# Two attention layers and two mixture-of-experts layers on one core: the first attention's values as one full-precision product per half

## The chip, the cores and the metric

The kernel runs on one core of one Trainium2 chip. The metric is the device time of one launch in microseconds (us), taken as the median over several runs.

## What is computed

`x` has 1024 tokens of 128 numbers, the context 6404 rows of 96. Four residual layers follow each other, each behind a layer norm of `x`: attention 0 (one head of 128), a mixture of 8 small experts, attention 1 (8 heads of 64, then an output projection), and a mixture of 32 experts with 4 chosen per token and one shared. What matters here is attention 0:

```python
query = jnp.einsum('bqi,ih->bqh', image_features, Wq) + bq
key = jnp.einsum('bkt,th->bkh', text_features, Wk) + bk
value = jnp.einsum('bkt,th->bkh', text_features, Wv) + bv
scores = jnp.einsum('bqh,bkh->bqk', query, key) * scale
weights = jax.nn.softmax(scores, axis=-1)
attended = jnp.einsum('bqk,bkh->bqh', weights, value)
...
x = x + _L0_xattn_ref(_layernorm(x, axis=-1), ctx_768, ...)
```

## The kernel before, in words

Each engine has its own instruction stream, written out by hand and tied to the others by semaphores; there is no scheduler. The context's 6404 rows are padded to 51 tiles (`TILES`) of 126 keys (`KT`), in 17 chunks (`CHUNKS`) of 3 (`CH`). The 1024 queries are two halves of 512 columns.

**Attention 0** never forms keys or values. The query is carried back through Wk (so a score is a product of a context row of 96 with the carried query), and the probabilities are summed against the context rows themselves plus a column of ones (97 numbers: 96 sums and the denominator). Wv is applied once at the end. Its steps in time:

1. A first pass over all tiles finds each query's maximum, and in its gaps makes the values of attention 1 and writes them to DRAM.
2. The second pass, the subject here (0 to 51 tiles, us 97 to 244 of the trace). For tile `j` of a chunk and each half of 512 queries:
   - `scores0` (L1174): three one-pass products in the reduced format float32r (L1180 to L1182), high and low parts of context and query, into PSUM bank `2j + half`.
   - `exp0` (L577) on ScalarE: the exponential in full float32 into `probs0`; `exp0_hi` (L586): the same exponential again, rounded to float32r, into `p_hi`.
   - `context_rows_hi` (L817) on VectorE: the tile's rows, loaded by the SyncE queue into `vslot`, rounded into `rows_hi`. GpSimd subtracts to `rows_lo` (L467). `probs_lo` (L822) on VectorE: `probs0 - p_hi` into `p_lo`.
   - `attend0` (L1185): three one-pass products, `rows_hi` by `p_hi`, `rows_lo` by `p_hi`, `rows_hi` by `p_lo`, added into banks 6 and 7.
   - `fill0` (L800) copies the keys of the same slot's next tile; the SyncE queue (L380) loads the slot's next rows as soon as `rows_lo` is made.
3. TensorE's order within a chunk is `chunk0` (L1202): scores of tile 2, attend 0, scores of the next chunk's tile 0, attend 1, scores of the next 1, attend 2. So a tile's scores stand two attends and two scores ahead of its own attend.

`p_hi` and `p_lo` have one buffer each for all tiles. They lie in the memory of `q_all2` and `q_shift2`, `rows_hi` and `rows_lo` in that of `wv1_hi` and `wv1_lo`; so the profile calls them `q_all`, `q_shift`, `wv_hi`, `wv_lo`, and `probs0` `probs`.

A float32 matmul of 512 columns is one instruction in the program and two records in the profile; one in float32r or bf16 is one of each.

Behind the pass come the division by the denominator, mixture 0 (us 244 to 296), the first keys and maxima of attention 1 (to us 381), its 8 heads (to us 1350), and mixture 1.

Of the kernel before, what the change touches and what calls it, by code (L numbers as in the profile page):

```python
# [6 lines left out]
F32R = mybir.dt.float32r  # L7
BF16 = mybir.dt.bfloat16
U32 = mybir.dt.uint32
ALU = mybir.AluOpType  # L10
ACT = mybir.ActivationFunctionType
AX = mybir.AxisListType.X

P = 128
TOK = 1024
TT = TOK // P
HALF = TOK // 2
D = 128
KEYS = 6404
CD = 96  # L20
KT = 126
TILES = 51
CH = 3
CHUNKS = TILES // CH
# [96 lines left out]
def build_program(nc, x, ctx_rows, ctx_t, a_wq, a_bq, a_wkt, a_bk, a_wv, a_bv,  # L121
# [4 lines left out]
    with ExitStack() as ctx:  # L126
# [6 lines left out]
        def sems(name, n):  # L133
            return [sem(f"{name}{i}") for i in range(n)]
# [3 lines left out]
        ps = ctx.enter_context(nc.psum_tensor("ps", [P, 8, HALF], F32))  # L138
# [42 lines left out]
        slot_keys, attended = sems("slot_keys", CH), sems("attended", CH)  # L181
        scored, exped = sems("scored", 2 * CH), sems("exped", 2 * CH)
# [5 lines left out]
                                    "o", "out", "rsum", "x"))  # L188


        a_plo0, a_av0 = sems("a_plo0", CH), sems("a_av0", CH)
        a_vkeys = sems("a_vkeys", CH)
        a_cslot, a_vproj, a_vevac, a_vout = (sems(f"a_{n}", CH) for n in ("cslot", "vproj", "vevac", "vout"))

# [11 lines left out]
        c_scored, c_exped, c_attended, c_sum, c_sumd = (  # L206
            sem(f"c_{n}") for n in ("scored", "exped", "attended", "sum", "sumd"))
        c_acc, c_sums, c_rden, c_out, c_x, c_bo = (sem(f"c_{n}") for n in ("acc", "sums", "rden", "out", "x", "bo"))
        a_lo, a_padd = sems("a_lo", CH), sems("a_padd", CH)

        g_step, g_logits, g_exp, g_cw, g_cwt, g_cwtsb, g_spread_ready, g_store = (
            sem(f"g_{n}") for n in ("step", "logits", "exp", "cw", "cwt", "cwtsb", "spread_ready", "store"))
# [33 lines left out]
        with ExitStack() as first:  # L246
            def sb_a(name, shape, dt=F32):
                return first.enter_context(nc.sbuf_tensor(name, shape, dt))

            keys_hl = sb_a("keys_hl", [P, TILES, 2, KT], F32R)  # L250
            kslot = sb_a("kslot", [P, CH, 2, KT], F32R)
            vslot = sb_a("vslot", [KT, CH, P])
            probs0 = sb_a("probs0", [KT, CH, TOK])
            q_max = sb_a("q_max", [P, TOK], F32R)
            q_all2 = sb_a("q_all2", [P, 2, TOK], F32R)
            q_shift2 = sb_a("q_shift2", [P, 2, TOK], F32R)
            q_pad = sb_a("q_pad", [97, TOK], F32R)
            wv1_hi = sb_a("wv1_hi", [P, HEADS * HD], F32R)
            wv1_lo = sb_a("wv1_lo", [P, HEADS * HD], F32R)
            v_stage = sb_a("v_stage", [KT, CH, HALF])  # L260
            chunk_max0 = sb_a("chunk_max0", [P, TT, CHUNKS])
            wq0 = sb_a("wq0", [P, D])
            bq0 = sb_a("bq0", [P, 1])
            wkt0 = sb_a("wkt0", [P, CD + 1])
            wv0 = sb_a("wv0", [CD + 1, D + 1])
            rsum0 = sb_a("rsum0", [P, 4, 2])
            xn2 = sb_a("xn2", [P, TT, D])
            f0w = sb_a("f0w", [P, 3 * 256 + 8 * 3 + 2 + 2 + 8 * 8])
            w2_0 = sb_a("w2_0", [P, G0, D])
            b2_0 = sb_a("b2_0", [E0, D])  # L270
            spread0 = sb_a("spread0", [E0, G0, P])
            mask0 = sb_a("mask0", [P, TT, E0])
# [6 lines left out]
        b1_0 = f0w[:, 792:794]  # L279
        hb0 = f0w[:, 794:796]  # L280
        lg0 = f0w[:, 796:860]
        q_all, q_shift = q_all2[:, 0, :], q_shift2[:, 0, :]
        p_hi, p_lo = q_all2[0:KT, 1, :], q_shift2[0:KT, 1, :]
        rows_hi, rows_lo = (w[0:KT, 0:CH * P].rearrange("p (j c) -> p j c", j=CH)[:, :, 0:CD + 1] for w in (wv1_hi, wv1_lo))

        with ExitStack() as second:
            def sb_b(name, shape, dt=F32):
# [32 lines left out]
        def f32(ap):  # L320
            return ap.bitcast(F32)
# [4 lines left out]
        def cols(half):  # L326
            return slice(half * HALF, (half + 1) * HALF)
# [16 lines left out]
        def _(sp):  # L344
# [26 lines left out]
            with sp.Fori(0, CHUNKS) as g:  # L371
                k1 = sp.snap(g + 1)
# [4 lines left out]
            with sp.Fori(0, CHUNKS - 1) as g:  # L377
                k1 = sp.snap(g + 1)
                for j in range(CH):
                    sp.wait_ge(a_lo[j], k1)  # L380
                    sp.dma_start(vslot[:, j, 0:CD],
                                 crow_v[bass.ds(g * CH + CH + j, 1)].rearrange("a p c -> p (a c)")).then_inc(a_cslot[j], 16)
            for j in range(CH):
# [46 lines left out]
        def _(pool):  # L430
# [25 lines left out]
            pool.tensor_copy(q_shift[0:CD, :], f32(q_max[0:CD, :])).then_inc(a_qcopy, 1)  # L456
            pool.wait_ge(a_qcopy, 1)
            pool.tensor_copy(q_pad[0:CD, :], f32(q_max[0:CD, :])).then_inc(a_qcopy, 1)

            pool.wait_ge(a_qcopy, 2)  # L460
            with pool.Fori(0, CHUNKS) as g:
                vkeys = pool.snap(g + (CHUNKS + 1))
                k1 = pool.snap(g + 1)
                for j in range(CH):
                    pool.wait_ge(a_vkeys[j], vkeys)
                    pool.wait_ge(a_lo[(j - 1) % CH], k1 if j else g)
                    pool.tensor_tensor(rows_lo[:, j, :], vslot[:, j, 0:CD + 1], f32(rows_hi[:, j, :]),  # L467
                                       ALU.subtract).then_inc(a_lo[j], 1)

            pool.wait_ge(attended[CH - 1], CHUNKS)  # L470

# [55 lines left out]
        def _(act):  # L527
# [38 lines left out]
            with act.Fori(0, CHUNKS - 1) as g:  # L566
                k1 = act.snap(g + 1)
# [7 lines left out]
                v_evac(j, CHUNKS, 16 * (CHUNKS - 1))  # L575

            def exp0(jj, kv, kp):  # L577

                act.wait_ge(a_padd[jj], kp)
                act.wait_ge(a_plo0[jj], kp)  # L580
                for half in range(2):
                    u = 2 * jj + half
                    act.wait_ge(scored[u], kv)
                    act.activation(probs0[:, jj, cols(half)], ps[0:KT, u, :], ACT.Exp, scale=float(D) ** -0.5)  # L584

            def exp0_hi(jj, kv, kp):  # L586

                for half in range(2):
                    u = 2 * jj + half
                    act.wait_ge((a_av0, attended)[half][(jj - 1) % CH], kv if jj else kp)  # L590
                    act.activation(p_hi[:, cols(half)], ps[0:KT, u, :], ACT.Exp,  # L591
                                   scale=float(D) ** -0.5).then_inc(exped[u], 1)

            def exp_tiles(k, k1, k2):
                exp0(1, k1, k)
                exp0_hi(0, k1, k)
                exp0(2, k1, k)
                exp0_hi(1, k1, k)
                if k2 is not None:
                    exp0(0, k2, k1)  # L600
                exp0_hi(2, k1, k)

            exp0(0, 1, 0)
            with act.Fori(0, CHUNKS - 1) as g:
                exp_tiles(g, act.snap(g + 1), act.snap(g + 2))
            exp_tiles(CHUNKS - 1, CHUNKS, None)
            act.wait_ge(attended[CH - 1], CHUNKS)
            act.copy(o0[:, 0:HALF], ps[0:CD + 1, 6, :]).then_inc(a_o, 1)

# [147 lines left out]
        def _(dve):  # L757
# [56 lines left out]
            dve.tensor_tensor(halves(q_shift[CD:CD + 1, :]), ps[CD:CD + 1, 3:5, :], halves(f32(q_max[CD:CD + 1, :])),  # L814
                              ALU.add).then_inc(shifted, 1)

            def context_rows_hi(j, k, k16):  # L817
                dve.wait_ge(a_cslot[j], k16)
                dve.wait_ge(attended[j], k)
                dve.tensor_copy(rows_hi[:, j, :], vslot[:, j, 0:CD + 1]).then_inc(a_vkeys[j], 1)  # L820

            def probs_lo(j, k1):  # L822
                for half in range(2):
                    dve.wait_ge(exped[2 * j + half], k1)
                    dve.tensor_tensor(p_lo[:, cols(half)], probs0[:, j, cols(half)], f32(p_hi[:, cols(half)]),  # L825
                                      ALU.subtract).then_inc((a_plo0, a_padd)[half][j], 1)

            with dve.Fori(0, CHUNKS - 1) as g:
                k1 = dve.snap(g + 1)
                n1 = dve.snap(g * CH + CH)  # L830
                k16 = dve.snap(g * 16 + 16)
                for j in range(CH):
                    context_rows_hi(j, g, k16)
                    probs_lo(j, k1)
                    dve.wait_ge(scored[2 * j + 1], k1)
                    fill0(n1 + j, j)
            for j in range(CH):
                context_rows_hi(j, CHUNKS - 1, 16 * CHUNKS)
                probs_lo(j, CHUNKS)
            dve.wait_ge(attended[CH - 1], CHUNKS)  # L840
            dve.tensor_copy(o0[:, HALF:TOK], ps[0:CD + 1, 7, :]).then_inc(a_o, 1)

# [277 lines left out]
        def _(pe):  # L1120
# [61 lines left out]
                    pe.matmul(s, kslot[0:CD + 1, jj, 1, :], q_pad[0:CD + 1, cols(half)], start=False,  # L1182
                              stop=True).then_inc(scored[u], 1)

            def attend0(j, k1):  # L1185

                pe.wait_ge(a_lo[j], k1)
                for half in range(2):
                    o = ps[0:CD + 1, 6 + half, :]
                    pe.wait_ge((a_plo0, a_padd)[half][j], k1)  # L1190
                    pe.matmul(o, rows_hi[:, j, :], p_hi[:, cols(half)], start=False, stop=False, skip_group_check=True)  # L1191
                    pe.matmul(o, rows_lo[:, j, :], p_hi[:, cols(half)], start=False, stop=False, skip_group_check=True)  # L1192
                    pe.matmul(o, rows_hi[:, j, :], p_lo[:, cols(half)], start=False, stop=False,  # L1193
                              skip_group_check=True).then_inc((a_av0, attended)[half][j], 1)

            pe.wait_ge(shifted, 1)
            pe.wait_ge(a_qcopy, 2)
# [1 line left out]
            pe.wait_ge(a_vevac[CH - 1], CHUNKS)  # L1199


            def chunk0(k, k1, k2):  # L1202
                scores0(2, k1, k)
                attend0(0, k1)
                if k2 is not None:
                    scores0(0, k2, k1)
                attend0(1, k1)
                if k2 is not None:
                    scores0(1, k2, k1)
                attend0(2, k1)  # L1210

            scores0(0, 1, 0)
            scores0(1, 1, 0)
            with pe.Fori(0, CHUNKS - 1) as g:
                chunk0(g, pe.snap(g + 1), pe.snap(g + 2))
            chunk0(CHUNKS - 1, CHUNKS, None)
            pe.wait_ge(a_o, 2)
            for t in range(TT):
                ins = pe.matmul(ps[:, t % 4, (t // 4) * 256:(t // 4) * 256 + D + 1], o0[:, tile_cols(t)], wv0[:, :],
# [383 lines left out]
```

## Time and profile before

| | |
|---|---|
| median of 3 runs | 1484.18 us (1483.55 to 1486.12) |
| the profiled execution's own time | 1484.28 us |
| its span in the profile | 1482.5 us (1.8 us lie around it) |
| TensorE busy | 1396.7 us, 94% of the span |
| VectorE, ScalarE, GpSimd busy | 1111.0, 807.6, 938.7 us |
| mean granted TensorE clock | 0.949 of full speed |
| the pass in question, us 97 to 244 | 147.0 us: TensorE busy 143.3, ScalarE 123.1, VectorE 87.1, GpSimd 20.8 |

A busy matmul record is longer than the time that it keeps the next one waiting, since the next streams in while it drains: the pace of a run of matmuls is the distance between their starts. The shares are averages over stages; what a change in one stage is worth is read in that stage. The granted clock is a share of full speed: 1.00 is 2.4 GHz, 0.50 is 1.2 GHz.

### The profile page before, as it was taken

To read this page: it belongs to the slowest core of one execution; us is meant where nothing else is said; L and a number is where in the kernel's file an instruction comes from. 1 tells how busy PE (TensorE), PEld (TensorE's weight loads), DVE (VectorE), ACT (ScalarE), POOL (GpSimd) and SP (SyncE) were. 2 spreads that over 40 slices of the span, in tenths; PEclk is the share of its full clock that TensorE was granted. 3 is DMA by queue.
4 is the path that set the end of the run, shared out by engine and by line. 5 is a ranking of instruction groups with operands and counts; after the bars stand their busy time and mean duration, and the time that the engine had idled before them with its cause. 6 is when DMAs were issued, how large, how long until landed. Compare 5 with 4: busy or idle time off the path is not lost.

```text
span 1482.5 us, 20192 instructions
## 1 busy us (share of the span) xinstructions
PE 1396.7 (94%) x6199; PEld 791.9 (53%) x6199; DVE 1111.0 (75%) x1518; ACT 807.6 (54%) x1625; POOL 938.7 (63%) x512
## 2 busy tenths in 40 slices
PE   4989996878999999999999999999999999997798
PEld 2867774533455545554555555555555555554465
DVE  6976567479779688778868877887887886766755
ACT  3768884232556556555655655665555555454232
POOL 5001115022689888978988898898898899885110
PEclk9999998565899999999999999999999999998799
DMA  6640000040000200020020011002002000000011
GB/s 158 208 134 17 17 17 7 1 91 2 1 1 1 49 1 1 1 49 1 1 48 1 1 28 22 0 1 49 0 1 45 1 1 1 1 1 13 19 37 39
DMA packets 77371, 39.42 MB, mean 27 GB/s; under 512 B 62047, under 2 KB 70000, under 8 KB 77002
## 3 DMA queue, kind: packets, MB, share of 16 engines
q1 hardware_dynamic: 77290, 38.36, 10.5%
q8 instruction: 49, 0.80, 0.2%
q14 instruction: 32, 0.26, 0.1%
HBM read 24.66 MB, written 13.68 MB: 26 GB/s over the span
## 4 chain that ended last, share of the span: by engine, by line
PE 86%; DVE 7%; DMA 3%; ACT 2%; issue 1%; POOL 0%; SPq 0%; ACTq 0%; DVEq 0%; POOLq 0%
PE ps L1348 24%; PE ps L1335 14%; PE ps L1336 12%; PE ps L1301 9%; PE ps L1288 3%; DMA v_scratch<-v_stage 2%; DVE chunk_max L921 2%; PE ps L1491 2%; PE ps L1191 2%; PE ps L1192 2%; PE ps L1193 2%; PE ps L1182 2%; PE ps L1180 2%; PE ps L1181 2%; PE ps L1280 1%
## 5 line engine op out<-in xcount | busy, mean ns | idle before, releaser
L506 POOL TENSOR_TENSOR psums<-psums,probs 126x1024 f32<-126x1024 f32 (+1 forms) x392 | 820.9, 2094 | 123.4 <-ACT probs L689 74.5
L689 ACT ACTIVATE probs<-ps 126x512 f32<-126x512 f32 (+1 forms) x816 | 416.4, 617 | 273.4 <-PE ps L1336 267.5
L921 DVE TENSOR_REDUCE chunk_max<-ps 128x2 f32<-128x1008 f32 (+1 forms) x416 | 472.9, 1180 | 79.5 <-PE ps L1301 77.9
L1348 PE MATMUL ps<-probs,v_mem 126*64 126x512 f32 (+1 forms) x1632 | 389.7, 598 | 0.0
L1335 PE MATMUL ps<-q_heads,ring 128*126 128x512 f32 (+1 forms) x816 | 342.9, 420 | 1.2
L1336 PE MATMUL ps<-q_low,ring 128*126 128x512 f32 (+1 forms) x816 | 322.5, 395 | 0.0
L974 DVE TENSOR_TENSOR xn<-xn,probs 126x512 f32<-126x512 f32 x126 | 230.6, 1830 | 29.9 <-ACT probs L689 25.6
L648 ACT CAST ring<-ps 64x252 fp32r<-64x252 f32 (+1 forms) x356 | 128.3, 360 | 135.9 <-PE ps L1288 132.8
L1348 PEld LDWEIGHTS ps<-probs,v_mem 126*64 126x64 f32 (+1 forms) x1632 | 111.5, 136 | 165.4 <-issue 121.2
L1335 PEld LDWEIGHTS ps<-q_heads,ring 128*126 128x126 f32 (+1 forms) x816 | 152.1, 186 | 88.8 <-issue 44.2
L1301 PE MATMUL ps<-ring,q_heads 64*128 64x504 f32 (+1 forms) x416 | 168.5, 477 | 15.8 <-DVE chunk_max L921 6.7
L1336 PEld LDWEIGHTS ps<-q_low,ring 128*126 128x126 f32 (+1 forms) x816 | 152.9, 187 | 32.6 <-issue 2.9
L1301 PE MATMUL ps<-ring,q_low 64*128 64x504 f32 (+1 forms) x416 | 168.5, 477 | 0.0
L1301 PEld LDWEIGHTS ps<-ring,q_heads 64*128 64x128 f32 x416 | 70.8, 197 | 159.1 <-issue 70.9
L467 POOL TENSOR_TENSOR wv_lo<-vslot,wv_hi 126x97 fp32r<-126x97 f32 x51 | 20.4, 399 | 190.7 <-DVE wv_hi L820 190.7
L825 DVE TENSOR_TENSOR q_shift<-probs,q_all 126x512 fp32r<-126x512 f32 x102 | 70.5, 692 | 58.8 <-ACT q_all L591 58.6
L911 DVE TENSOR_TENSOR ring<-ps,ring 64x252 fp32r<-64x252 f32 (+1 forms) x178 | 73.7, 414 | 34.6 <-ACT ring L648 32.4
L1301 PEld LDWEIGHTS ps<-ring,q_low 64*128 64x128 f32 x416 | 70.7, 197 | 0.0
L591 ACT ACTIVATE q_all<-ps 126x512 fp32r<-126x512 f32 x102 | 60.9, 599 | 11.1 <-PE ps L1193 1.4
L584 ACT ACTIVATE probs<-ps 126x512 f32<-126x512 f32 x102 | 60.7, 600 | 9.7 <-PE ps L1182 2.9
L515 POOL TENSOR_TENSOR parts<-pair_w,parts 128x256 fp32r<-128x256 f32 x17 | 11.7, 693 | 83.4 <-ACT parts L715 83.4
L795 DVE TENSOR_REDUCE chunk_max<-ps 128x1 f32<-128x378 f32 x136 | 62.7, 539 | 2.0 <-PE ps L1153 2.0
(200 smaller groups left out, 1456.7 us busy)
## 6 DMA issues: line engine op xcount, KB each, us to landing
v_scratch<-v_stage SPq DMA_DIRECT2D x51, 252.0 KB
v_mem<-v_scratch SPq DMA_DIRECT2D x8, 1606.5 KB
ctx_mem<-in_ctx_t SPq DMA_DIRECT2D x3, 803.2 KB, 9.3
vslot<-in_ctx_rows SPq DMA_DIRECT2D x51, 47.2 KB
pair_w<-in_f_pairs SPq DMA_DIRECT2D x17, 128.0 KB, 2.1
pair_w<-in_f_pairs SPq DMA_DIRECT2D x17, 65.0 KB, 1.8
x_tok<-in_x SPq DMA_DIRECT2D x1, 512.0 KB, 3.6
wo<-in_c_wo SPq DMA_DIRECT2D x1, 512.0 KB
```

The costliest lines, as they stand in the source:

```text
L506: pool.tensor_tensor(sums[0:r, 0:width], sums[0:r, 0:width], probs[0:r, n % PROBS, 0:width], ALU.add).then_inc(c_sum, 1)
L648: ins = act.copy(ring[half * HD:(half + 1) * HD, g % RING, tiles, 0, :], ps[part * HD:(part + 1) * HD, bank, 0:(tiles.stop - tiles.start) ...
L689: act.activation(probs[0:r, n % PROBS, cols(half)], ps[0:r, score_bank(t, half), :], ACT.Exp, scale=float(HD) ** -0.5).then_inc(c_exped, 1)
L795: dve.tensor_reduce(chunk_max0[:, i, g:g + 1], ps[:, i % 4, 0:CK], AX, ALU.max).then_inc(max_reduced, 1)
L825: dve.tensor_tensor(p_lo[:, cols(half)], probs0[:, j, cols(half)], f32(p_hi[:, cols(half)]), ALU.subtract).then_inc((a_plo0, a_padd)[half] ...
L911: ins = dve.tensor_tensor(ring[HD:P, g % RING, tiles, 1, :], ps[rows, bank, 0:(tiles.stop - tiles.start) * KT] .rearrange("p (n k) -> p n ...
L921: dve.tensor_reduce(chunk_max[:, h % 2, i:i + 2, c], ps[:, banks[0]:banks[1] + 1, 0:group_tiles(c) * KT], AX, ALU.max).then_inc(c_reduced, 1)
L974: dve.tensor_tensor(sums[0:r, :], sums[0:r, :], new[0:r, :], ALU.add).then_inc(c_sumd, 1)
L1301: pe.matmul(ps[:, banks[half], 0:group_tiles(c) * KT], q[rows, h % 3, tile_cols(i + half)], ring[rows, g % RING, 0:group_tiles(c), 0, :], ...
L1335: pe.matmul(s, ring[:, g % RING, j, 0, 0:r], q_heads[:, h % 3, cols(half)], start=True, stop=False)
L1336: pe.matmul(s, ring[:, g % RING, j, 1, 0:r], q_low[:, h % 3, cols(half)], start=False, stop=True).then_inc(c_scored, 1)
L1348: ins = pe.matmul(ps[half * HD:(half + 1) * HD, B_ACC, :], v_tiles[0:r, h % 2, t, :], probs[0:r, n % PROBS, cols(half)], start=(t == 0), s ...
```

## The change

The parts are gone. `attend0` is one float32 product per half, of `vslot` as loaded and `probs0` as the exponential left it. ScalarE takes each exponential once. VectorE's two roundings and subtractions per tile and GpSimd's subtraction go, with six sets of semaphores. The queue's reload of a slot now waits for that slot's `attended` where it waited for `a_lo`, and TensorE waits for the load itself (`a_cslot`) and for `exped`.

```diff
             with sp.Fori(0, CHUNKS - 1) as g:
                 for j in range(CH):
-                    sp.wait_ge(a_lo[j], k1)
+                    sp.wait_ge(attended[j], k1)
                     sp.dma_start(vslot[:, j, 0:CD], ...
...
-            with pool.Fori(0, CHUNKS) as g:
-                for j in range(CH):
-                    pool.wait_ge(a_vkeys[j], vkeys)
-                    pool.wait_ge(a_lo[(j - 1) % CH], k1 if j else g)
-                    pool.tensor_tensor(rows_lo[:, j, :], vslot[:, j, 0:CD + 1], f32(rows_hi[:, j, :]),
-                                       ALU.subtract).then_inc(a_lo[j], 1)
...
             def exp0(jj, kv, kp):
-                act.wait_ge(a_padd[jj], kp)
-                act.wait_ge(a_plo0[jj], kp)
+                act.wait_ge(attended[jj], kp)
                 for half in range(2):
                     u = 2 * jj + half
                     act.wait_ge(scored[u], kv)
-                    act.activation(probs0[:, jj, cols(half)], ps[0:KT, u, :], ACT.Exp, scale=float(D) ** -0.5)
-            def exp0_hi(jj, kv, kp):
-                for half in range(2):
-                    act.wait_ge((a_av0, attended)[half][(jj - 1) % CH], kv if jj else kp)
-                    act.activation(p_hi[:, cols(half)], ps[0:KT, u, :], ACT.Exp,
+                    act.activation(probs0[:, jj, cols(half)], ps[0:KT, u, :], ACT.Exp,
                                    scale=float(D) ** -0.5).then_inc(exped[u], 1)
...
-            exp0(0, 1, 0)
-            with act.Fori(0, CHUNKS - 1) as g:
-                exp_tiles(g, act.snap(g + 1), act.snap(g + 2))
-            exp_tiles(CHUNKS - 1, CHUNKS, None)
+            with act.Fori(0, CHUNKS) as g:
+                k1 = act.snap(g + 1)
+                for j in range(CH):
+                    exp0(j, k1, g)
...
                 for j in range(CH):
-                    context_rows_hi(j, g, k16)
-                    probs_lo(j, k1)
                     dve.wait_ge(scored[2 * j + 1], k1)
                     fill0(n1 + j, j)
...
-            def attend0(j, k1):
-                pe.wait_ge(a_lo[j], k1)
+            def attend0(j, k1, k16):
+                pe.wait_ge(a_cslot[j], k16)
                 for half in range(2):
-                    o = ps[0:CD + 1, 6 + half, :]
-                    pe.wait_ge((a_plo0, a_padd)[half][j], k1)
-                    pe.matmul(o, rows_hi[:, j, :], p_hi[:, cols(half)], start=False, stop=False, skip_group_check=True)
-                    pe.matmul(o, rows_lo[:, j, :], p_hi[:, cols(half)], start=False, stop=False, skip_group_check=True)
-                    pe.matmul(o, rows_hi[:, j, :], p_lo[:, cols(half)], start=False, stop=False,
-                              skip_group_check=True).then_inc((a_av0, attended)[half][j], 1)
+                    pe.wait_ge(exped[2 * j + half], k1)
+                    ins = pe.matmul(ps[0:CD + 1, 6 + half, :], vslot[:, j, 0:CD + 1], probs0[:, j, cols(half)], start=False,
+                                    stop=False, skip_group_check=True)
+                ins.then_inc(attended[j], 1)
```

On TensorE, in the loop over chunks, the first attend of a chunk stood so before (between the scores of tile 2 and those of the next chunk's tile 0; `q_all` is `p_hi`, `q_shift` is `p_lo`, in brackets the semaphores waited for):

```order
L1191 MATMUL ps<-q_all,wv_hi 97x512 [waits a_plo00,a_lo0]
L1192 MATMUL ps<-q_all,wv_lo 97x512
L1193 MATMUL ps<-q_shift,wv_hi 97x512
L1191 MATMUL ps<-q_all,wv_hi 97x512 [waits a_padd0]
L1192 MATMUL ps<-q_all,wv_lo 97x512
L1193 MATMUL ps<-q_shift,wv_hi 97x512
```

and so with the change, scores of tile 2's second half ahead of it and the next scores behind:

```order
L1130 MATMUL ps<-q_shift,kslot 126x512 [waits exped5]
L1131 MATMUL ps<-q_all,kslot 126x512
L1132 MATMUL ps<-q_pad,kslot 126x512
L1136 ISA
L1139 MATMUL ps<-probs,vslot 97x512 [waits exped0,a_cslot0]
L1139 MATMUL ps<-probs,vslot 97x512 [waits exped1]
L1125 REGISTER_ALU
L1130 MATMUL ps<-q_shift,kslot 126x512 [waits exped0,slot_keys0]
```

Six matmuls of one attend have become two; the order of scores and attends is the same.

On ScalarE, before, from the end of the first pass into the loop (`L604` is the loop's head, the rows of L584 write `probs0`, those of L591 `p_hi`):

```order
L584 ACT_TABLE_LOAD
L584 ACTIVATE probs<-ps 126x512 x2
L604 UNCONDITIONAL_BRANCH
L583 REGISTER_ALU
L584 ACTIVATE probs<-ps 126x512 x2
L591 ACTIVATE q_all<-ps 126x512 x2
L584 ACTIVATE probs<-ps 126x512 x2
L591 ACTIVATE q_all<-ps 126x512 x2
```

and with the change, from the loop's head to its branch back:

```order
L570 UNCONDITIONAL_BRANCH
L566 REGISTER_ALU
L567 ACT_TABLE_LOAD
L567 ACTIVATE probs<-ps 126x512 x6
L570 REGISTER_ALU
L570 COMPARE_AND_BRANCH
```

Twelve exponentials per chunk have become six, and the load of the exponential's table has moved from ahead of the loop into it.

## Rows read from the trace of the kernel before

**Rows 1.** Stretches of the second pass: us, each engine's busy us (records), clock, DMA.
```profile
97.00:244.00 147.00, 143.33 (x612) 106.61 (x612) 87.05 (x203) 123.11 (x206) 20.78 (x52) 1.00 0.07 16
...
103.10:238.70 135.60, 135.59 (x582) 101.47 (x582) 82.44 (x195) 116.09 (x195) 19.56 (x49) 1.00 0.07 17
```
**Rows 2.** Groups by line, us 97 to 244: busy us, mean ns, then idle before.
```profile
L825 DVE TENSOR_TENSOR q_shift<-probs,q_all 126x512 fp32r<-126x512 f32 x102 | 70.5, 692 | 58.8 <-ACT q_all L591 58.6
L591 ACT ACTIVATE q_all<-ps 126x512 fp32r<-126x512 f32 x102 | 60.9, 599 | 11.1 <-PE ps L1193 1.4
L584 ACT ACTIVATE probs<-ps 126x512 f32<-126x512 f32 x102 | 60.7, 600 | 9.7 <-PE ps L1182 2.9
...
L1180 PE MATMUL ps<-q_shift,kslot 97*126 97x512 f32 x102 | 40.3, 395 | 1.6 <-DVE q_shift L814 1.6
L1191 PE MATMUL ps<-q_all,wv_hi 126*97 126x512 f32 x102 | 40.3, 395 | 2.9 <-DVE q_shift L825 2.9
...
L467 POOL TENSOR_TENSOR wv_lo<-vslot,wv_hi 126x97 fp32r<-126x97 f32 x51 | 20.4, 399 | 190.7 <-DVE wv_hi L820 190.7
```
**Rows 3.** Instructions in order of time, TensorE, first products of attends: start us, us.
```profile
111.43 0.39 PE L1191 MATMUL ps<-q_all,wv_hi 126*97 126x512 f32 x1
...
225.96 0.39 PE L1191 MATMUL ps<-q_all,wv_hi 126*97 126x512 f32 x1
...
228.75 0.39 PE L1191 MATMUL ps<-q_all,wv_hi 126*97 126x512 f32 x1
```
**Rows 4.** The same view, TensorE in mixture 1's loop: L1491 is float32.
```profile
1421.07 0.39 PE L1486 MATMUL ps<-cw,spread 96*128 96x512 bf16 x1
1421.30 1.02 PE L1491 MATMUL ps<-hgate,pair_w 128*128 128x512 f32 x2
...
1422.40 0.40 PE L1479 MATMUL ps<-parts 128*128 128x512 f32 x1
...
1428.73 1.02 PE L1491 MATMUL ps<-hgate,pair_w 128*128 128x512 f32 x2
```
**Rows 5.** The same view, TensorE in attention 1's last head.
```profile
1316.76 3.65 PE L1348 MATMUL ps<-probs,v_mem 126*64 126x512 f32 x16
...
1324.25 1.08 PE L1348 MATMUL ps<-probs,v_mem 126*64 126x512 f32 x4
```
**Rows 6.** Waits in the pass (total, times, longest); then its start in order of time.
```profile
PE ps L1191 <- DVE q_shift L825: 2.9, 3, 1.3
...
98.31 1.28 ACT L584 ACT_TABLE_LOAD   x1 [3.68 <-PE ps L1182]
...
99.61 2.06 ACT L584 ACTIVATE probs<-ps 126x512 f32<-126x512 f32 x4
...
101.31 0.39 PE L1182 MATMUL ps<-q_pad,kslot 97*126 97x512 f32 x1
```
**Rows 7.** DMA issues of the page: count, KB each, median us to landing.
```profile
wq<-in_c_wq SPq DMA_DIRECT2D x8, 64.0 KB, 9.6
...
wk<-in_c_wk SPq DMA_DIRECT2D x8, 48.0 KB, 2.9
```
**Rows 8.** Stretches behind the pass, TensorE: us, busy (records), granted clock, DMA.
```profile
272.00:279.00 7.00, 6.55 (x21) 0.99 0.01 1
...
327.00:381.00 54.00, 47.24 (x110) 0.50 0.01 1
381.00:1350.00 969.00, 962.06 (x4574) 1.00 0.06 12
```
**Rows 9.** The chain that ended last, behind the pass: start us, us.
```profile
268.79 3.54 PE ps L1243 x4
...
273.21 1.72 PE ps L1243 x4
...
279.41 1.22 PE ps L1261 x4
...
293.75 0.74 PE ps L1262 x2
```

More of the change, by code:

```diff
@@ L188, in build_program @@
                                     "o", "out", "rsum", "x"))
-        a_plo0, a_av0 = sems("a_plo0", CH), sems("a_av0", CH)
         a_vkeys = sems("a_vkeys", CH)
@@ L208, in build_program @@
         c_acc, c_sums, c_rden, c_out, c_x, c_bo = (sem(f"c_{n}") for n in ("acc", "sums", "rden", "out", "x", "bo"))
-        a_lo, a_padd = sems("a_lo", CH), sems("a_padd", CH)
         g_step, g_logits, g_exp, g_cw, g_cwt, g_cwtsb, g_spread_ready, g_store = (
@@ L254, in build_program @@
             q_max = sb_a("q_max", [P, TOK], F32R)
-            q_all2 = sb_a("q_all2", [P, 2, TOK], F32R)
-            q_shift2 = sb_a("q_shift2", [P, 2, TOK], F32R)
+            q_all = sb_a("q_all", [P, TOK], F32R)
+            q_shift = sb_a("q_shift", [P, TOK], F32R)
             q_pad = sb_a("q_pad", [97, TOK], F32R)
@@ L281, in build_program @@
         lg0 = f0w[:, 796:860]
-        q_all, q_shift = q_all2[:, 0, :], q_shift2[:, 0, :]
-        p_hi, p_lo = q_all2[0:KT, 1, :], q_shift2[0:KT, 1, :]
-        rows_hi, rows_lo = (w[0:KT, 0:CH * P].rearrange("p (j c) -> p j c", j=CH)[:, :, 0:CD + 1] for w in (wv1_hi, wv1_lo))
         with ExitStack() as second:
@@ L458, in _ @@
             pool.tensor_copy(q_pad[0:CD, :], f32(q_max[0:CD, :])).then_inc(a_qcopy, 1)
-            pool.wait_ge(a_qcopy, 2)
-            with pool.Fori(0, CHUNKS) as g:
-                vkeys = pool.snap(g + (CHUNKS + 1))
-                k1 = pool.snap(g + 1)
-                for j in range(CH):
-                    pool.wait_ge(a_vkeys[j], vkeys)
-                    pool.wait_ge(a_lo[(j - 1) % CH], k1 if j else g)
-                    pool.tensor_tensor(rows_lo[:, j, :], vslot[:, j, 0:CD + 1], f32(rows_hi[:, j, :]),
-                                       ALU.subtract).then_inc(a_lo[j], 1)
             pool.wait_ge(attended[CH - 1], CHUNKS)
@@ L583, in exp0 @@
                     act.wait_ge(scored[u], kv)
-                    act.activation(probs0[:, jj, cols(half)], ps[0:KT, u, :], ACT.Exp, scale=float(D) ** -0.5)
-            def exp0_hi(jj, kv, kp):
-                for half in range(2):
-                    u = 2 * jj + half
-                    act.wait_ge((a_av0, attended)[half][(jj - 1) % CH], kv if jj else kp)
-                    act.activation(p_hi[:, cols(half)], ps[0:KT, u, :], ACT.Exp,
-                                   scale=float(D) ** -0.5).then_inc(exped[u], 1)
[L594 to L601, printed above, removed]
-            exp0(0, 1, 0)
-            with act.Fori(0, CHUNKS - 1) as g:
-                exp_tiles(g, act.snap(g + 1), act.snap(g + 2))
-            exp_tiles(CHUNKS - 1, CHUNKS, None)
+                    act.activation(probs0[:, jj, cols(half)], ps[0:KT, u, :], ACT.Exp,
+                                   scale=float(D) ** -0.5).then_inc(exped[u], 1)
+            with act.Fori(0, CHUNKS) as g:
+                k1 = act.snap(g + 1)
+                for j in range(CH):
+                    exp0(j, k1, g)
             act.wait_ge(attended[CH - 1], CHUNKS)
@@ L815, in _ @@
                               ALU.add).then_inc(shifted, 1)
[L817 to L826, printed above, removed]
             with dve.Fori(0, CHUNKS - 1) as g:
@@ L830, in _ @@
                 n1 = dve.snap(g * CH + CH)
-                k16 = dve.snap(g * 16 + 16)
                 for j in range(CH):
-                    context_rows_hi(j, g, k16)
-                    probs_lo(j, k1)
                     dve.wait_ge(scored[2 * j + 1], k1)
                     fill0(n1 + j, j)
-            for j in range(CH):
-                context_rows_hi(j, CHUNKS - 1, 16 * CHUNKS)
-                probs_lo(j, CHUNKS)
             dve.wait_ge(attended[CH - 1], CHUNKS)
@@ L1199, in _, with chunk0 @@
             pe.wait_ge(a_vevac[CH - 1], CHUNKS)
-            def chunk0(k, k1, k2):
+            def chunk0(k, k1, k2, k16):
                 scores0(2, k1, k)
-                attend0(0, k1)
+                attend0(0, k1, k16)
                 if k2 is not None:
                     scores0(0, k2, k1)
-                attend0(1, k1)
+                attend0(1, k1, k16)
                 if k2 is not None:
                     scores0(1, k2, k1)
-                attend0(2, k1)
+                attend0(2, k1, k16)
             scores0(0, 1, 0)
@@ L1214, in _ @@
             with pe.Fori(0, CHUNKS - 1) as g:
-                chunk0(g, pe.snap(g + 1), pe.snap(g + 2))
-            chunk0(CHUNKS - 1, CHUNKS, None)
+                chunk0(g, pe.snap(g + 1), pe.snap(g + 2), pe.snap(g * 16 + 16))
+            chunk0(CHUNKS - 1, CHUNKS, None, 16 * CHUNKS)
             pe.wait_ge(a_o, 2)
```

## The prediction

> **What bounds the kernel now.** I read the stretches of the program first. From us 97 to 244, the only part that the diff touches, TensorE is busy 143.3 of 147.0 us at a granted clock of 1.00; in the inner 135.6 us it is busy 135.59 [rows 1]. ScalarE has 123.1 and VectorE 87.1 in the same stretch, so both have air, GpSimd nearly all. The groups by line then say why ScalarE is that full: 102 exponentials at 600 ns, twice [rows 2]. But those are work beside TensorE's, and what ends last is a matmul. The order of time gives TensorE's pace: the first products of two following attends start at 225.96 and 228.75, 2.79 us apart, and 111.43 to 225.96 is 114.53 us for 41 tiles, 2.793 us each [rows 3]. A tile is 12 one-pass products of 512 columns, so one costs 2.793 / 12 = 0.2328 us. (The 395 ns of the groups [rows 2] hold the drain, which the next product covers.) A pass with no gap at one product per 0.233 us is bound by the count of products, and by nothing that ScalarE, VectorE or GpSimd do.
>
> **The change, part by part.**
>
> *The three products of a half become one float32 product.* Removed per tile: 6 x 0.2328 = 1.397 us of TensorE. Added: two float32 products of 512 columns. The trace has the price in the loop of mixture 1, at full clock: L1491 is one float32 matmul, two records. From its start at 1421.30 to the same at 1428.73 are three rounds, 2.477 us each, and a round has 7 one-pass products and this one [rows 4]: 2.477 - 7 x 0.2328 = 0.85 us, entry and exit included. It is no cheaper than 3.6 one-pass products, where the change takes out 3. The other place is attention 1: eight float32 matmuls in four pairs, a pair side by side in the two column halves of the array, then 16 one-pass products; block to block is 1324.25 - 1316.76 = 7.49 us [rows 5]. That leaves 7.49 - 16 x 0.2328 = 3.77 us, 0.94 per pair, with what it costs to change between half and full columns. Nothing in the trace has exactly 126 rows by 97 columns in float32 at full clock. Bounds are therefore 0.85 and 0.94. I take 0.85: L1491 uses the whole array, as the new product does, has one-pass products on both sides, as here, and the new product splits no columns.
> Per tile 2 x 0.85 - 1.397 = +0.303 us; over 51 tiles **+15.5 us**, all on the path since TensorE has no gap there. (With 0.94: +24.7 us.)
>
> The Trainium skill, "Perfetto Trace Analysis", section Engine Utilization, gives TensorE's output rate as halved for its FP32_LOW_HIGH; read as the whole price of a float32 product, it would make one cost two one-pass products, and the sum would be below zero (rival B). Its page "FP8 and Floating Point Precision", TensorE Precision Notes, says true FP32 takes four passes through the array; at the pace above that is 4 x 0.2328 = 0.93 us, and the sum would be some +20.8 us; the row of 0.85 stands under it and is used.
>
> *The gaps at the ends.* TensorE waits for `p_lo` three times, 2.9 us in all: once in the first attend, where the last score product starts at 101.31 and the attend not before 103.03, and twice among the last three tiles, where no scores stand between [rows 6]. After the change the first attend needs the rows (loaded long before) and two exponentials. The table load starts at 98.31, the exponentials at 99.61, two take 1.3 us, and so they are done by 100.9, before the last score product is through. In the last chunk an attend of 1.7 us is longer than the two exponentials of the next tile. Both gaps go: **-2.9 us**.
>
> *ScalarE.* 102 exponentials of 0.60 us less. Added: the table load is inside the loop now, 17 times instead of once, 1.28 us each [rows 6]. A chunk then has 1.28 + 6 x 0.65 = 5.2 us of ScalarE against 3 x 3.10 = 9.3 us of TensorE. The load comes behind the wait for the slot's `attended`, ahead of tile 0's exponentials. TensorE needs those after two attends and two groups of scores, 2 x 1.7 + 2 x 1.4 = 6.2 us from the end of tile 0's scores; load and two exponentials are 2.6 us, with one earlier exponential ahead 3.2. Hidden, 3 us to spare: 0. Without that cover it would be 16 x 1.28 = 20.5 us.
>
> *VectorE and GpSimd.* 70.5 us of `p_lo`, the roundings of rows, 20.4 us of `rows_lo` [rows 2], all beside TensorE: 0. VectorE's `fill0` no longer stands behind `p_lo`, so keys come earlier. GpSimd goes straight to its wait for the last attend.
>
> *The rows' load.* It was issued when `rows_lo` was made, ahead of the attend; now when the attend is through, and TensorE waits for its landing. The slot is wanted again 9.3 - 1.7 = 7.6 us after its attend ends, less about 0.4 us for the queue's issue: it must land within 7.2 us. The trace has no landing for these 47 KB. The nearest rows are 48 KB in 2.9 us and 64 KB in 9.6 us [rows 7]; the latter are issued around loads of 1.6 MB, of which the pass has none (DMA share 0.07 [rows 1]). I take 2.9: hidden, 0. By 9.6 it would be rival C.
>
> *Behind the pass.* Nothing is changed, but it begins some 13 us later, and TensorE's clock there comes and goes: 0.99 in us 272 to 279, 0.50 in 327 to 381, 1.00 from 381 on [rows 8]. The same four records of L1243 are 3.54 us at the lower level (1.2 GHz) and 1.72 at the upper (2.4 GHz) [rows 9]. Where the clock rises need not move with the work. Lost, the fast stretch would cost some 6 us; had the small matmuls from 279.41 to 294.5 [rows 9] been fast, some 7 us would be gained. I take 0 and keep -7 and +6 for the range.
>
> Sum against the profiled execution: 1484.28 + 15.5 - 2.9 = 1496.9, say **1497.0 us**. That execution lies 0.1 us from the median of the runs, so nothing is corrected. About 0.2% (3 us) is what a measurement of this kernel can tell from no change.
>
> **The rivals.**
>
> B, *the float32 product is cheap*: one costs two one-pass products (0.47 us), as the half rate named above would have it. A tile falls from 12 to 10 products of 0.2328 us: 51 x -0.466 = -23.7, with the gaps -26.6: 1457.7 us. This is the case on the other side. It decides where a float32 product costs under 0.70 us, three one-pass ones. For it speaks only that every other engine would let it happen (ScalarE 5.2 us per chunk). Against: two records per matmul and 0.85 us [rows 4], and 3.77 us for four pairs [rows 5]. 2%.
>
> C, *the rows land late*: at 9.6 us a slot's turn is 1.7 + 0.4 + 9.6 = 11.7 us instead of 9.3, over 16 chunks +38 us: about 1535. It decides from a landing of 7.2 us. Against it the DMA engines stand nearly idle. 2%.
>
> D, *dearer change of kind*: the price of attention 1's blocks, 0.94 us, holds here. +24.7 - 2.9 = +21.8: 1506.1 us. For it: that block has the 126 rows and `probs` as moving operand, as here. Against: its halves of columns. 9%.
>
> E, *the clock behind the pass pays it back*: it must give 9.6 us or more for no change; even the fast small matmuls give only 7. It would take those and parts of us 327 to 381, where VectorE bounds half of the chain. Time about 1487, or less: 3%, of which I count 2 within 0.2% and 1 beyond.
>
> That the change does not do what it says can be left out: the order of TensorE has two matmuls for six. The forecast itself has 84%.
>
> **How the numbers follow.** Predicted is the likeliest case, 1497.0. Downwards the clock gives up to 5 us within the range, as a full 7 is unlikely; upwards D's price ends at 1506. So 1492 to 1506 leaves out B, C, E and the joint worst of D and clock, under 2 in 10. Faster by over 0.2%: B and a part of E, 3%. Within 0.2%: 2%. Slower by over 0.2%: 95%.
>
> **What would show it.** In the changed profile: 102 float32 products of `probs` and `vslot` in 204 records; first records of following attends 3.10 us apart, 9.3 us per chunk; the pass from us 97 to about 256; no TensorE idle before an attend; ScalarE with 17 table loads and about 83 us busy in the pass; VectorE some 15 us, GpSimd none. A round of 3.28 us is D, of 3.9 us with a wait for `vslot` is C, of 2.33 is B. If the round is 3.10 and the total is off by more than 3 us, the time lies behind the pass, in the rows of the granted clock. A wait for ScalarE once per chunk would be the table load.

## The result, and the profile after

The change takes 1500.41 us (median of 4 runs, 1498.9 to 1501.85) against 1484.76 us before (median of 4, 1483.55 to 1486.12). The ratio is 1.0097, with a 95% interval of 1.0080 to 1.0114: slower by 1%. The forecast was 1497.0 us, in a range of 1492 to 1506.

The groups by line of the changed kernel, us 97 to 262 (busy us, mean ns of a record, idle before and what ended it), answer to [rows 2]:

```profile
L1139 PE MATMUL ps<-probs,vslot 126*97 126x512 f32 x204 | 95.6, 591 | 0.0
L1130 PE MATMUL ps<-q_shift,kslot 97*126 97x512 f32 x102 | 59.7, 585 | 1.6 <-DVE q_shift L781 1.6
L567 ACT ACTIVATE probs<-ps 126x512 f32<-126x512 f32 x102 | 59.2, 596 | 57.4 <-PE ps L1132 55.7
...
L567 ACT ACT_TABLE_LOAD x17 | 21.8, 1283 | 19.0 <-PE ps L1139 18.9
```

102 float32 products in 204 records, 17 table loads, and no idle time of TensorE before an attend. The stretches (us; TensorE, its weight loads, VectorE, ScalarE, GpSimd busy; clock; DMA) answer to [rows 1]:

```profile
103.10:250.00 146.90, 146.90 (x472) 84.03 (x471) 13.45 (x46) 75.22 (x112) 0.00 (x0) 1.00 0.07 16
...
97.00:262.00 165.00, 161.90 (x533) 93.22 (x530) 18.12 (x58) 82.04 (x121) 3.80 (x2) 1.00 0.07 17
```

In the inner stretch TensorE is without a gap, as before. Over the whole window VectorE fell from 87.1 to 18.1 us and ScalarE from 123.1 to 82.0, and GpSimd has nothing left in the inner stretch; none of it made the round shorter. (The window, us 97 to 262, holds 4 us behind the pass.) The order of time, TensorE and one table load on ScalarE, answers to [rows 3]:

```profile
226.69 1.28 ACT L567 ACT_TABLE_LOAD   x1 [1.18 <-PE ps L1139]
...
227.82 1.88 PE L1139 MATMUL ps<-probs,vslot 126*97 126x512 f32 x4
227.98 1.09 ACT L567 ACTIVATE probs<-ps 126x512 f32<-126x512 f32 x2
...
229.14 0.80 PE L1130 MATMUL ps<-q_shift,kslot 97*126 97x512 f32 x1
229.78 0.40 PE L1131 MATMUL ps<-q_all,kslot 96*126 96x512 f32 x1
...
230.94 1.88 PE L1139 MATMUL ps<-probs,vslot 126*97 126x512 f32 x4
...
237.17 1.88 PE L1139 MATMUL ps<-probs,vslot 126*97 126x512 f32 x4
```

Attends start at 227.82, 230.94, (234.06) and 237.17: 9.35 us for three tiles, 3.117 each, where it was 2.793. Less six one-pass products, 1.397, that leaves 1.720 for two float32 products: **0.860 us each**. The first score product behind an attend has a long record (0.80 us): it starts at 229.14, while the attend's records still run (to 227.82 + 1.88 = 229.70), and the next product follows 0.64 us behind it, not 0.23. So part of the float32 product's time stands in that record, and the 585 ns a record of L1130's group are no cost of its own.

### The profile page after: what moved, and what is told of

It is laid out like the page before. It is cut to its first block, busy times and chain, and to the rows that moved or that the text cites. A ratio compares the mean times of both kernels' runs of the same rounds, so it can differ in the third digit from the quotient of the medians.

```text
span 1497.1 us, 19515 instructions
## 1 busy us (share of the span) xinstructions
PE 1412.1 (94%) x6097; PEld 776.6 (52%) x6097; DVE 1035.3 (69%) x1365; ACT 764.8 (51%) x1539; POOL 919.8 (61%) x461
## 4 chain that ended last, share of the span: by engine, by line
PE 87%; DVE 8%; DMA 3%; ACT 2%; issue 1%; POOL 0%; SPq 0%; ACTq 0%; DVEq 0%; POOLq 0%
PE ps L1295 24%; PE ps L1282 14%; PE ps L1283 12%; PE ps L1248 9%; PE ps L1139 6%; PE ps L1235 2%; DMA v_scratch<-v_stage 2%; DVE chunk_max L871 2%; PE ps L1438 2%; PE ps L1130 2%; PE ps L1132 2%; PE ps L1131 2%; PE ps L1227 1%; PE ps L1220 1%; PE ps L1427 1%
## 5 line engine op out<-in xcount | busy, mean ns | idle before, releaser
L1248 PEld LDWEIGHTS ps<-ring,q_heads 64*128 64x128 f32 x416 | 70.7, 197 | 159.3 <-issue 69.3
L768 DVE CAST kslot<-keys_hl 97x252 fp32r (+1 forms) x51 | 14.7, 292 | 131.2 <-PE ps L1132 131.2
L1139 PE MATMUL ps<-probs,vslot 126*97 126x512 f32 x204 | 95.6, 591 | 0.0
```

The costliest lines, as they stand in the source:

```text
L1139: ins = pe.matmul(ps[0:CD + 1, 6 + half, :], vslot[:, j, 0:CD + 1], probs0[:, j, cols(half)], start=False, stop=False, skip_group_check=True)
L1248: pe.matmul(ps[:, banks[half], 0:group_tiles(c) * KT], q[rows, h % 3, tile_cols(i + half)], ring[rows, g % RING, 0:group_tiles(c), 0, :], ...
```

## The experiments

For every profile the table gives the pass, from its first score product to the copy of its sum out of PSUM, and the rest of the span, all in us. The medians of the group from change_again to three_products stand against 1486.13 us of the kernel before, run beside them, those of the group from late_reload on against 1485.97.

| kernel | pass starts | length | rest of the span | median us |
|---|---|---|---|---|
| before | 97.2 | 146.3 | 1336.2 | 1484.76 |
| the change | 98.8 | 159.3 | 1337.8 | 1500.41 |
| change_again | 99.2 | 159.3 | 1338.1 | 1500.57 |
| product_only | 98.8 | 163.4 | 1337.8 | 1502.38 |
| load_hoisted | 97.7 | 159.3 | 1338.8 | 1499.29 |
| three_products | 99.6 | 204.9 | 1340.8 | 1546.63 |
| late_reload | 98.6 | 199.9 | 1339.8 | 1541.54 (one run) |
| two_one_pass | 99.4 | 119.0 | 1337.1 | 1459.71 |
| one_one_pass | 98.4 | 95.2 | 1336.2 | 1434.23 |
| one_one_pass_hoisted | 99.3 | 95.2 | 1337.2 | 1434.54 |

**The product alone.** From the kernel before:

```diff
-                    pe.matmul(o, rows_hi[:, j, :], p_hi[:, cols(half)], start=False, stop=False, skip_group_check=True)
-                    pe.matmul(o, rows_lo[:, j, :], p_hi[:, cols(half)], start=False, stop=False, skip_group_check=True)
-                    pe.matmul(o, rows_hi[:, j, :], p_lo[:, cols(half)], start=False, stop=False,
+                    pe.matmul(o, vslot[:, j, 0:CD + 1], probs0[:, j, cols(half)], start=False, stop=False,
...
```

and the queue's reload waits for `attended[j]`. The other engines go on making the parts, which nothing uses.

> The kernel before with the float32 product alone: both exponentials, the roundings and the subtractions on ScalarE, VectorE and GpSimd stay and the order of waits too; only the parts' three products per half become one float32 product, and the rows' reload waits for the attend. Theory 1 (TensorE's stream alone sets the pass): 51 x 2 x (0.858 - 0.698) = +16.3 us, and of the 2.9 us of gaps some 2.5 stay: about +16 us against the kernel before, a round of 3.12 us per tile. Theory 2 (part of the cost comes from the thinner waits, the table load or the load that is waited for, and the other engines' relief is worth something): clearly other than +16, either under +10 or over +20. The output is that of the change; the parts are computed and not used.

Measured: ratio to before 1.0105 (1.0088 to 1.0122), +16.3 us between medians. The round is 3.12 us, since attends start at 227.05, 230.16 and 233.28 us, in the order of time of TensorE:

```profile
227.05 1.88 PE L1191 MATMUL ps<-probs,vslot 126*97 126x512 f32 x4
230.16 1.88 PE L1191 MATMUL ps<-probs,vslot 126*97 126x512 f32 x4
233.28 1.88 PE L1191 MATMUL ps<-probs,vslot 126*97 126x512 f32 x4
...
257.63 1.93 PE L1191 MATMUL ps<-probs,vslot 126*97 126x512 f32 x4 [0.65 <-DVE q_shift L825]
260.21 1.93 PE L1191 MATMUL ps<-probs,vslot 126*97 126x512 f32 x4 [0.65 <-DVE q_shift L825]
```

The last two rows are gaps of [rows 6], 0.65 us each now; with the first attend's 0.59 the idle time is 1.9 us, not the 2.5 expected. What the gaps cost is more, counted from start to start: the last score product starts at 104.43 and the attend at 105.41, 0.75 us more than a product takes, and the last three attends start 2.52 and 2.58 us apart where two float32 products are 1.72. Together that is 2.4 us. So the product alone makes the whole loss and more, and all the work taken from the three other engines is worth only these gaps. The pass is 4.1 us longer than the change's: 2.4 are the gaps, and 1.6 lie at its start, where the granted clock was low (last section). Between the medians are 1.8 us.

**A third product.** In the change, the first half's product is issued twice, which doubles its sum and its denominator alike:

```diff
                     pe.wait_ge(exped[2 * j + half], k1)
-                    ins = pe.matmul(ps[0:CD + 1, 6 + half, :], vslot[:, j, 0:CD + 1], probs0[:, j, cols(half)], start=False,
-                                    stop=False, skip_group_check=True)
+                    for again in range(2 - half):
+                        ins = pe.matmul(ps[0:CD + 1, 6 + half, :], vslot[:, j, 0:CD + 1], probs0[:, j, cols(half)],
+                                        start=False, stop=False, skip_group_check=True)
```

> The change with the first half's float32 product issued twice per tile (its sum is then doubled, so the output is another). It prices one float32 product in its place. Theory 1: 51 x 0.858 = +43.8 us against the change, a round of 3.97 us. Theory 2 (the price holds a cost of changing between float32r and float32, 0.19 us per tile, which a product more doesn't pay): a further product costs 0.853 or less while the pair costs more than 1.72 us together. Rival price 0.94: +48 us.

Measured: +46.1 us between the medians of this and of change_again. The order of time, TensorE, gives the price free of what lies around the loop:

```profile
224.90 2.74 PE L1140 MATMUL ps<-probs,vslot 126*97 126x512 f32 x6
...
228.87 2.74 PE L1140 MATMUL ps<-probs,vslot 126*97 126x512 f32 x6
...
232.85 1.45 PE L1140 MATMUL ps<-probs,vslot 126*97 126x512 f32 x3
```

A round is 3.975 us (232.85 is the next attend's start), 0.858 more than with two: the third product costs as much as each of the first two. There is no cost of changing between the formats in the pair, and rival D falls: its 0.94 us does not hold here. That it belongs to attention 1's column halves is likely, and was not tried. Of the 46.1 us 43.8 are the rounds; the pass is 45.6 longer, with a stretch of low clock at its start (some 1.6 us), which the change's profiles do not have.

**The table load outside the loop.** In the change:

```diff
-            with act.Fori(0, CHUNKS) as g:
-                k1 = act.snap(g + 1)
-                for j in range(CH):
-                    exp0(j, k1, g)
+            exp0(0, 1, 0)
+            with act.Fori(0, CHUNKS - 1) as g:
+                k1 = act.snap(g + 1)
+                exp0(1, k1, g)
+                exp0(2, k1, g)
+                exp0(0, act.snap(g + 2), k1)
+            exp0(1, CHUNKS, CHUNKS - 1)
+            exp0(2, CHUNKS, CHUNKS - 1)
```

> The change with the first exponential taken out of ScalarE's loop, so that the exponential's table is loaded once and not 17 times. Theory 1 (the load is hidden, 3 us to spare): equal to the change within 1 us, round 3.12 us per tile, ScalarE 20.5 us less busy. Theory 2 (once per chunk the load delays an attend): up to 16 x 1.28 = 20 us less than the change.

Measured: 1499.29 against 1500.57 us of change_again. That is 1.3 us where 1 was expected at most, and within the runs' own spread (1497.34 to 1502.11 here); in the profiles the pass is 159.3 us, the same to the tenth, and starts 1.1 to 1.5 us earlier than in the two of the change. The load was hidden.

**The change again.**

> The change as it is, for the spread of its runs and for the start of the second pass, which its first profile had 1.55 us later (98.80 against 97.25 us). If the late start is chance among the writes of the values in the first pass, this profile's start lies anywhere from 97 to 99 us and the ratio to before comes to 1.0085 to 1.0105. If it belongs to the change, the start is 98.5 to 99 again.

Measured: 1500.57 us, ratio 1.0118 (1.0079 to 1.0158). One of its six runs took 1518.84 us and lifts the ratio above what was expected; between the medians are 14.4 us, 1.0097. The pass starts at 99.18 us and is 159.3 long. The start is 0.18 us later than either expectation allowed, and so fits neither. Over all ten profiles, whose first pass is the same code, the start lies anywhere from 97.2 to 99.6 us; load_hoisted, which is the change but for the table load, starts at 97.7, and other kernels than the change start late too. So the late start does not belong to the change. What goes with it is the granted clock in us 28 to 40, long before the pass that the edits touch (us, TensorE busy, clock, DMA), here before and in the change:

```profile
28.00:40.00 12.00, 11.21 (x46) 0.86 0.36 118
...
28.00:40.00 12.00, 11.91 (x44) 0.76 0.34 112
```

The four profiles with 0.86 there (before, load_hoisted, late_reload, one_one_pass) start the pass at 97.2 to 98.6 us, the six with 0.72 to 0.76 at 98.8 to 99.6. That one makes the other was not tried. The one profile of before had the earliest start of the ten.

**A late reload.** In the change, a slot's reload waits two attends longer:

```diff
-                k1 = sp.snap(g + 1)
+                k1, k2 = sp.snap(g + 1), sp.snap(g + 2)
                 for j in range(CH):
-                    sp.wait_ge(attended[j], k1)
+                    sp.wait_ge(attended[(j + 2) % CH], k2 if j else k1)
```

> The change with a slot's reload issued only after the attend of the slot used last before it, two attends later than in the change. The rows then land on TensorE's path every tile, and the wait shows how long a load of 47 KB takes. A tile is 1.72 us of attend, some 0.45 us of the queue's issue and the landing. Theory 1 (as 48 KB in 2.9 us): about 5.1 us per tile, 48 x 2.0 = +95 us against the change, so that in the change the rows land over 4 us before they are wanted. Rival C (as 64 KB in 9.6 us): 11.8 us per tile, +415 us, and the change would then have waited for its rows. Nothing is left out.

Measured in a single run: 1541.54 us, a pass 40.6 us longer. The order of time shows one turn: the attend before ends at 227.44 + 0.59 = 228.03, the queue issues at 228.23 (the row holds that issue and the next three), TensorE starts on the rows at 229.98 and had waited for the DMA:

```profile
227.44 0.59 PE L1139 MATMUL ps<-probs,vslot 126*97 126x512 f32 x1
...
228.23 12.02 SPq L376 DMA_DIRECT2D vslot<-in_ctx_rows  x4
...
229.98 1.96 PE L1139 MATMUL ps<-probs,vslot 126*97 126x512 f32 x4 [0.54 <-DMA vslot<-in_ctx_rows]
...
233.88 1.96 PE L1139 MATMUL ps<-probs,vslot 126*97 126x512 f32 x4 [0.55 <-DMA vslot<-in_ctx_rows]
```

From issue to use are 1.75 us, and a tile is 3.90 us. That is shorter than either bound I had (2.9 and 9.6 us of landing), so where +95 us was expected it came to +41. In the change the rows have 7.6 us and need some 2: they are over 5 us early, and rival C falls.

**Fewer products.** From the kernel before: the exponential once, as in the change, but written as float32r; `probs_lo` gone; `rows_hi` and `rows_lo` kept; and in `attend0`

```diff
                 for half in range(2):
                     pe.wait_ge(exped[2 * j + half], k1)
                     ins = pe.matmul(ps[0:CD + 1, 6 + half, :], rows_hi[:, j, :], probs0[:, j, cols(half)], ...
+                    ins = pe.matmul(ps[0:CD + 1, 6 + half, :], rows_lo[:, j, :], probs0[:, j, cols(half)], ...
                 ins.then_inc(attended[j], 1)
```

with the added line in two_one_pass and without it in one_one_pass. Both are other computations than before: the first leaves out the probabilities' low part, the second the rows' as well.

> From the kernel before: one exponential per half, rounded to float32r as it is written; rows in high and low part as before; the attend is two one-pass products per half (high rows, low rows), without the probabilities' low part. That low part is left out of the computation, in numerator and denominator alike. Theory 1 (only TensorE's count of streamed columns): 10 products a tile, 2.33 us, 51 x -0.466 = -23.7 and -2.9 of gaps, 1458 to 1460 us. Theory 2 (something else of the change holds the pass near 3.1 us a tile, ScalarE's chain or the rows): no faster than the change, about 1500.

> As two_one_pass, with only the product of the high rows by the rounded probabilities: 8 products a tile. Both low parts are left out of the computation. Theory 1: 1.86 us a tile, 51 x -0.931 = -47.5 and -2.9 of gaps, about 1435 us. Rival: ScalarE, with the table load in its loop 5.2 us per chunk against TensorE's 5.6, begins to hold the pass; then TensorE shows idle before an attend once per chunk and the time lies 5 to 20 us above 1435.

> As one_one_pass, with the first exponential outside ScalarE's loop, so one table load instead of 17. If the load is hidden there too, equal within 1 us; if it holds the pass, this one is up to 16 x 1.28 = 20 us faster than one_one_pass.

Measured: two_one_pass 1459.71 us, ratio to before 0.9828 (0.9810 to 0.9847); one_one_pass 1434.23, ratio 0.9652 (0.9635 to 0.9669); hoisted 1434.54, ratio 0.9663 (0.9637 to 0.9689). The stretch of two_one_pass's whole pass, and two attends of one_one_pass with a table load between them (order of time):

```profile
99.40:218.40 119.00, 118.95 (x510) 90.46 (x510) 24.72 (x100) 79.80 (x119) 20.28 (x51) 1.00 0.09 20
```

```profile
152.88 0.62 PE L1164 MATMUL ps<-probs,wv_hi 126*97 126x512 f32 x2
...
153.69 1.28 ACT L582 ACT_TABLE_LOAD   x1
...
154.75 0.63 PE L1164 MATMUL ps<-probs,wv_hi 126*97 126x512 f32 x2
```

The passes are 119.0 and 95.2 us. By the count, 51 x 10 and 51 x 8 products of 0.2328 us are 118.7 and 95.0, so the pass has nothing left but TensorE's stream, and this holds down to a round of 1.87 us (152.88 to 154.75). In one_one_pass ScalarE is busy 4.8 us of a chunk of 5.6 (expected 5.2), and the table load still costs nothing: the hoisted form has the same pass, and neither shows a wait of TensorE for ScalarE. Both times lie where theory 1 had them, and the rivals are not seen. one_one_pass is 66 us faster than the change and 52 faster than before, and two_one_pass 41 and 26; what they pay for it is those low parts.

## Why the prediction was right, step by step

*What bounds the pass.* Right: TensorE busy 146.90 of 146.90 us after, and kernels with 8, 10 and 12 one-pass products a tile, or two or three float32 ones in place of six, all follow the sum of their products, but for the gaps and stretches of low clock told above.

*The price of a float32 product.* I took 0.85 us from the loop of mixture 1 [rows 4], against a bound of 0.94 [rows 5]. Measured 0.860 in the change and 0.858 for a third one. Per tile +0.324 instead of +0.303, over the pass +16.5 instead of +15.5 us. Here lies the term that was short, by 1.0 us. The place with the same use of the array was the right one to take, and the half rate of the Trainium skill, "Perfetto Trace Analysis", section Engine Utilization, read as the price of a whole product, does not hold here: it would be 0.47 us, rival B. Read as the price of one record it fits: a product has two, and 0.860 / 2 = 0.43 us is near two products of 0.2328. The Trainium skill, "FP8 and Floating Point Precision", TensorE Precision Notes, has four passes for true FP32, and the price measured here fits that: 0.858 / 4 = 0.2145 us for each. The trace shows two records, not four passes.

*The gaps.* All three went, as the last attends show: twelve records of L1139 in one run of 5.32 us from 252.77. But 2.9 us, their idle time, was too small a price. Pass to pass the sum is 159.3 - 146.3 = +13.0 us, and +16.5 - 2.9 would be +13.6. The order of time before shows where 0.6 us are:

```profile
103.03 0.44 PE L1191 MATMUL ps<-q_all,wv_hi 126*97 126x512 f32 x1 [1.33 <-DVE q_shift L825]
...
238.29 0.40 PE L1193 MATMUL ps<-q_shift,wv_hi 126*97 126x512 f32 x1
239.49 0.44 PE L1191 MATMUL ps<-q_all,wv_hi 126*97 126x512 f32 x1 [0.80 <-DVE q_shift L825]
...
240.70 0.40 PE L1193 MATMUL ps<-q_shift,wv_hi 126*97 126x512 f32 x1
241.91 0.44 PE L1191 MATMUL ps<-q_all,wv_hi 126*97 126x512 f32 x1 [0.81 <-DVE q_shift L825]
```

Idle time is counted from the end of a record of 0.40 us, where the next product would have started after 0.23. From start to start, less one product, the three gaps are 1.72, 1.20 and 1.21 less 0.23 each, 3.4 us in all, and some 0.05 more each because the first product behind a gap holds up the next for 0.28 us. The passes say the same: 146.3 is 3.9 us over 51 x 2.793, 159.3 is 0.3 over 51 x 3.117, so the gaps gave back 3.5, and +16.5 - 3.5 = +13.0. The forecast's +12.6 lies so near because two terms were too small, the product by 1.0 and the gaps by 0.6, and their errors partly cancel. That is luck.

*Costed at nothing.* The table load (load_hoisted), the rows' load (late_reload) and the relief of VectorE and GpSimd beyond the gaps (product_only) were all worth nothing, as said. The landing itself I had too high.

*Behind the pass.* I took 0 and was afraid of -7 to +6. From the copy at the end of the pass to the end of the span are 1482.5 - 243.55 = 1238.95 us before and 1497.1 - 258.12 = 1238.98 in the change, 1238.91 in change_again: 0, and rival E falls. (Over all ten profiles it is 1237.7 to 1241.2. Rival E took VectorE to bound half of the chain in us 327 to 381; in the trace it has 30% of it.) The granted clock came again with the work, 15 us later: against 0.99 in us 272 to 279 [rows 8] the change has, in the same view,

```profile
287.00:294.00 7.00, 6.14 (x20) 0.95 0.00 0
...
342.00:396.00 54.00, 47.32 (x111) 0.50 0.01 2
396.00:1364.00 968.00, 961.01 (x4568) 1.00 0.06 12
```

*The rest of the miss.* The change's median is 3.4 us above the forecast. 0.4 are in the pass. 1.55 are its later start (98.80 against 97.25), in code that the change does not touch. Behind the pass is nothing. The last 1.5 are the distance from the change's profiled run, 1498.9 us, to its median; 0.1 went into rounding the forecast up. So 3 us are not a term of the change: I summed against one execution, 1484.28 us, with the earliest start of ten profiles. Later medians of the same kernel before are 1484.76, 1486.13 and 1485.97. In the same session the step is 1500.57 - 1486.13 = 14.4 us, in the first comparison 15.7, with intervals of 6 us and of 2.5 us to either side.

## What to carry to other kernels

Count what an edit streams through TensorE before counting what it saves elsewhere: where TensorE has no gap, a float32 product of 512 columns (0.858 us) is dearer than three one-pass products (0.698 us), and freeing a hundred microseconds of other engines buys only the waits that TensorE really had, 3.5 us. Price such a wait from start to start, less one product: its idle time alone was 0.6 us short here. With fewer one-pass products the same simplification pays, 26 and 52 us, for the low parts that are given up. When a sum is made against one profiled execution, its own luck is in the forecast: 3 us here, a fifth of the effect.

## What the runs showed that I had not expected

A quarter of a float32 product costs 0.2145 us, one product in float32r 0.2328 us, for the same 512 columns at a granted clock of 1.00. The lower level has a row for the same float32r product. In product_only six of them lie between these two starts, 2.56 us, 0.427 each:

```profile
99.68 0.63 PE L1180 MATMUL ps<-q_shift,kslot 97*126 97x512 f32 x1
...
102.24 0.63 PE L1180 MATMUL ps<-q_shift,kslot 97*126 97x512 f32 x1
```

Half of that is 0.2133 us. So at the full clock the quarter of a float32 product is about as fast as the clock alone would make it, and the one-pass products, each with weights of its own, lose 0.02 us. Why was not tried.

In two of the ten profiles, product_only and three_products, the second pass began at the lower clock level. The stretches of product_only (us, TensorE busy, granted clock, DMA) show it:

```profile
97.00:99.00 2.00, 0.21 (x2) 1.00 0.47 146
99.00:101.00 2.00, 2.00 (x7) 0.62 0.00 0
101.00:103.00 2.00, 2.00 (x6) 0.52 0.00 0
103.00:106.00 3.00, 2.41 (x10) 1.00 0.00 0
```

Ahead of it TensorE was nearly idle from 97.0 to 98.8 us. From the first score product to the last ahead of the first attend are 5.63 us (98.80 to 104.43) where the change has 4.08 (98.80 to 102.88): 1.55 us lost, and the same in three_products. But the change and change_again had a like stretch (0.43 and 0.18 us busy of us 97 to 99) and stayed at 1.00, so that the same point of near-identical programs may or may not lose 1.6 us. It was not tried whether work in that stretch would prevent it.
